# A constant matmul moved from the first to the last place of its accumulation chain

## The reference, cut to what matters

```
h   = max(layernorm(x), 0)                       # x: (64, 128, 128)
h_k = einsum('bjf,kfo->kbjo', h, W)              # W: (3, 128, 128)
out = adj_diag @ h_0 + adj_upper @ h_1 + adj_lower @ h_2 + bias
x   = x + out
```

## Time and profile before

| | us |
|---|---|
| median of 3 runs | 425.54 |
| lowest, highest | 425.4, 428.08 |
| the profiled execution | 425.69 |
| its span in the profile | 423.6 |
| TensorE busy | 408.0 |
| VectorE, ScalarE busy | 329.6, 279.7 |

### The profile page before, as it was taken

How to read it: one execution, slowest core, us unless ns; L and a number is a source line. 1 busy time by engine, 2 the same in 40 slices (tenths; PEclk the granted TensorE clock), 3 DMA queues, 4 the chain that set the end, 5 groups by cost and what they waited for, 6 DMA issues and landing times.

```text
span 423.6 us, 7808 instructions
## 1 busy us (share of the span) xinstructions
PE 408.0 (96%) x2594; PEld 365.4 (86%) x2594; DVE 329.6 (78%) x845; ACT 279.7 (66%) x566; POOL 47.7 (11%) x55
## 2 busy tenths in 40 slices
PE   8997989899999999999989999999999999999897
PEld 7785879898878899999868889999887889999787
DVE  5569898989886788797967678878888777767841
ACT  4667666775966576766776576677596676667542
POOL 3792002001100002000210001100110000000300
PEclk9998999999999999999999999999999999999999
DMA  7900000000001000000001000000000000000011
GB/s 218 373 32 0 2 0 2 1 2 0 2 19 39 14 0 15 1 20 2 0 2 38 31 0 12 1 19 0 1 2 19 27 0 14 0 20 0 13 52 63
DMA packets 6081, 11.17 MB, mean 26 GB/s; under 512 B 1056, under 2 KB 4768, under 8 KB 5536
## 3 DMA queue, kind: packets, MB, share of 16 engines
q1 hardware_dynamic: 6048, 10.77, 7.2%
HBM read 6.57 MB, written 4.19 MB: 25 GB/s over the span
## 4 chain that ended last, share of the span: by engine, by line
PE 82%; DVE 9%; ACT 4%; issue 2%; DMA 1%; POOL 1%; SPq 0%; DVEq 0%; ACTq 0%
PE PS L461 11%; PE PS L462 11%; PE PS L470 11%; PE PS L530 9%; PE PS L489 6%; PE PS L486 6%; PE PS L485 6%; PE PS L513 5%; PE PS L394 3%; PE PS L417 3%; PE PS L409 3%; PE PS L427 3%; ACT GT L709 2%; PE PS L499 1%; ACT TC L718 1%
## 5 line engine op out<-in xcount | busy, mean ns | idle before, releaser
L709 ACT ACTIVATE GT<-PS,BG 128x256 f32<-128x256 f32 (+2 forms) x312 | 158.8, 563 | 51.6 <-PE PS L489 28.2
L461 PE MATMUL PS<-HH,WIH 128*128 128x256 f32 (+2 forms) x312 | 108.8, 349 | 6.2 <-issue 2.9
L462 PE MATMUL PS<-HH,WIL 128*128 128x256 f32 (+2 forms) x312 | 103.3, 332 | 0.0
L470 PE MATMUL PS<-HL,WIH 128*128 128x256 f32 (+2 forms) x294 | 97.4, 331 | 0.3
L718 ACT ACTIVATE TC<-CS 128x512 f32<-128x512 f32 (+2 forms) x88 | 45.1, 512 | 45.9 <-DVE CS L829 29.5
L461 PEld LDWEIGHTS PS<-HH,WIH 128*128 128x128 f32 x312 | 59.2, 190 | 11.3 <-DVE HH L853 3.5
L320 POOL TENSOR_TENSOR RS<-VE,NHALF 128x8 f32<-128x8 f32 (+2 forms) x15 | 26.5, 1765 | 350.7 <-DVE VE L777 350.7
L462 PEld LDWEIGHTS PS<-HH,WIL 128*128 128x128 f32 x312 | 59.5, 191 | 3.5
L470 PEld LDWEIGHTS PS<-HL,WIH 128*128 128x128 f32 x294 | 55.6, 189 | 6.0 <-DVE HL L868 1.7
L489 PE MATMUL PS<-SL,WHH 128*128 128x256 f32 (+2 forms) x192 | 59.9, 312 | 0.0
L486 PE MATMUL PS<-SH,WHL 128*128 128x256 f32 (+2 forms) x192 | 59.8, 311 | 0.0
(11 more groups left out here) (85 smaller groups left out, 593.3 us busy)
## 6 DMA issues: line engine op xcount, KB each, us to landing
X<-x_tbd SPq DMA_DIRECT2D x3, 1024.0 KB, 11.6
out_tbd<-X SPq DMA_DIRECT2D x15, 192.0 KB, 1.9
X<-x_tbd SPq DMA_DIRECT2D x4, 256.0 KB, 4.4
WI<-wih_t SPq DMA_DIRECT2D x1, 1024.0 KB, 6.0
out_tbd<-X SPq DMA_DIRECT2D x7, 128.0 KB, 1.7
WH<-whh_t SPq DMA_DIRECT2D x1, 768.0 KB, 7.3
out_tbd<-X SPq DMA_DIRECT2D x1, 256.0 KB, 2.4
WL<-w_l SPq DMA_DIRECT2D x1, 192.0 KB, 7.0
```

Of the source, the lines that this page charges most:

```text
L461: pe.matmul(dst, WIH[:, p - 1, cols], x_high, start=True, stop=False)
L462: pe.matmul(dst, WIL[:, p - 1, cols], x_high, start=False, stop=False)
L470: mm = pe.matmul(dst, WIH[:, p - 1, cols], x_low, start=False, stop=(j == 0))
L709: act.activation(GT[:, s, q, 0:n], bank(s, q)[:, 0:n], ACT.Tanh if q == C else ACT.Sigmoid, bias=BG[:, 4 * (p - 1) + q:4 * (p - 1) + q + 1 ...
```

## The change

The bias matmul of a chunk is issued behind the chunk's last OUTP matmul instead of ahead of its first one. `start=True` goes to the first matmul of the chunk's first batch, and `out_mm` to the bias matmul. There are 24 bias matmuls in the program before and after, of the same shapes.

```diff
             def last_out(g, n, ps, plan):
 
                 c, first, last = chunk_of(plan, n)
-                if first:
+                pe.wait_ge(uk_sb, G * g + n + 1)
+                for k in range(ADJ_PARTS):
+                    pe.matmul(as_batches(ps)[:, n - plan.chunks[c][0], :], UK[:, n % 4, k * T:(k + 1) * T],
+                              WL1[:, k, :], start=(first and k == 0), stop=False, skip_group_check=True)
+                if last:
 
                     size = plan.chunks[c][1]
                     pe.matmul(as_batches(ps)[:, 0:size, :], TWO[:, :],
-                              BIAS2[:, :].unsqueeze(1).broadcast_to([T, size, D]), start=True, stop=False,
-                              skip_group_check=True)
-                pe.wait_ge(uk_sb, G * g + n + 1)
-                for k in range(ADJ_PARTS):
-                    mm = pe.matmul(as_batches(ps)[:, n - plan.chunks[c][0], :], UK[:, n % 4, k * T:(k + 1) * T],
-                                   WL1[:, k, :], start=False, stop=(k == ADJ_PARTS - 1), skip_group_check=True)
-                if last:
-                    mm.then_inc(out_mm, 1)
+                              BIAS2[:, :].unsqueeze(1).broadcast_to([T, size, D]), start=False, stop=True,
+                              skip_group_check=True).then_inc(out_mm, 1)
```

## The result

| | before | changed |
|---|---|---|
| median of 20 runs | 425.58 us | 427.31 us |
| lowest, highest | 424.74, 428.08 | 426.25, 429.79 |
| ratio of the times | | 1.0038 (95%: 1.0022 to 1.0054) |
| profiled execution, its span | 425.69, 423.6 | 429.79, 427.7 |

The changed kernel is 0.4% slower, 1.6 us, where 0.87 us was forecast: inside the stated range and inside 1%, but nearly twice the size. The interval of the ratio stands for 0.9 to 2.3 us. The profiled execution of the changed kernel happens to be its slowest, 4.1 us above that of before; 2.88 us of these are there before the first piece of the last layer is issued, where the two programs do the same. So the comparison has to be made from the first ADJP on.

What follows compares the result with a forecast made beforehand. TensorE was taken as the bound, busy 408.0 of 423.6 us. Chunk 4's 0.36, chunk 5's 0.51 and 0 elsewhere gave +0.87 us, 426.56 on the profiled execution and 426.4 us for the median; range 425.0 to 427.8 us.

Steps and rivals of the forecast that it cites:

- Chunk 4: Bias hidden in the wait before unit 9's gates becomes bare behind OUTP 12: 3 x 0.12 = +0.36 us.
- Chunk 5: Bias hidden by the wait ahead of ADJP 15 becomes bare behind OUTP 15: 3 x 0.17 = +0.51 us.
- Chunks 0 and 1: Chunk 0's bias loses its cover, +0.17 us; chunk 1's opening stall on the bank goes, -0.19 us; together taken as 0.
- Chunks 2 and 3, and LATE's single batch: Bias taken out and put back in the same dense TensorE stream: cost 0.
- The double wait: Matmul opening a chunk now waits for `out_ready` (or a gate's activation) and `uk_sb` at once: taken as 0, bound +1.1 us.
- The tail: Last group and LATE's last chunk: bias moves inside an idle stretch or a gapless TensorE stretch, cost 0.
- Nothing at all: Rival, chance 0.18: slack the chain does not show takes up the 0.29 us per group; 425.6 us.
- Faster: Rival, chance 0.12: chunk 1's stall goes (3 x 0.19), chunk 0's cover costs nothing, chunks 4 and 5 absorbed; 425.0 us.
- Slower by chunk 0: Rival, chance 0.14: chunk 0's bias loses cover and chunk 1's stall stays, 3 x 0.17 = 0.51 more; 426.9 us.
- slower by the double wait: Rival, chance 0.06: each chunk opening costs a step of 0.07 us, +1.1 + 0.87; 427.5 us.

Runs made afterwards that it cites:

- late chunks: Bias moved behind the chunk only in the two chunks per group issued in units 9 to 16 (6 of 24), against the kernel before: median 427.11 us, ratio 1.0011.
- the others: Bias moved behind the chunk in the other 18 of 24 matmuls only, against the kernel before: median 426.26 us, ratio 1.0009.
- leaving the matmuls out: Kernel before without 9 hidden bias matmuls (chunks 0, 4, 5; LATE 0, 3, 4): median 428.41 us; without 8 dense ones: 425.20 us.
- chunk 0 alone: Bias moved behind the chunk only in chunk 0 of each of the three groups, against the kernel before: median 428.04 us, ratio 1.0029.
- the filled kernels: Kernel before and changed kernel, each with unread matmuls (12 and 6) added in two TensorE waits of the first group: medians 425.36 and 426.46 us.

## Why the prediction was right or wrong

The direction held, and the mechanism held but for chunk 3 and LATE's single batch. A bias matmul that had filled a wait costs its full time at a place where TensorE is the chain, and one moved within a dense stretch costs nothing as long as nothing behind it was waiting under its cover; the split into late chunks and the others, and leaving the matmuls out, show it from both sides.

**Chunk 4**, +0.12 us in each group: measured 0.12 us, with the idle time at the old place grown from 0.23 to 0.34 us.

**Chunk 5**, +0.17 us in each group: the amount held (0.17 us), the place of the loss did not. I said that the wait ahead of ADJP 15 would grow. It stayed at 0.42 us, and the loss is at the first gate of unit 15, which waits for VectorE's HH and HL. In the trace of before these matmuls followed OUTP 13 with no idle time shown, since the bias had just about filled the gap. In group 3 the step is 0.20 us; the repeated trace of before differs by 0.03 us at this place.

**Chunks 0 and 1**, +0.17 and -0.19 us: measured +0.17, and -0.35 us at the opening of chunk 1, of which 0.17 us come back at its end. The start of ADJP 2 did not move at all. The run with chunk 0 alone gives +0.01 us in sum. VectorE's add stayed where it was (8.58 us), as I had said.

**Chunks 2 and 3, and LATE's single batch**, taken as 0: this term was mis-sized. It is 0.05 us for chunk 3 in each of two groups, since the copy of UK 10 was covered by the bias, and another 0.04 to 0.05 us at LATE's single batch. There my reading of the trace was wrong: the chain of before does not stay a bare 0.06 us in that bias (0.23 us scaled from 512 to 128 columns) but 0.29 us, with a wait for the bank in it.

```profile
329.63 0.29 PE PS L525
```

In the changed kernel this bias takes 0.06 us, and the gate matmul behind it 0.28 instead of 0.23 us; the opening waits as before. Leaving it out altogether was worth 0.05 us. That its cost was partly hidden in the wait fits these figures, but no run isolates it. For chunk 3 I had read the chunks as dense from the chain, which names only the engine; the margin of a copy against the OUTP that reads it has to be taken from the timeline of both engines. With the 384-column matmul at 0.18 instead of 0.17 us behind an fp32 matmul, the whole is 1.0 us without the step at group 2 instead of 0.87, and 1.10 us by the filled kernels.

**The double wait**, taken as 0: the changed program has 16 instructions more on its page (7,824 against 7,808), all of them EVENT_SEMAPHORE on TensorE (66 against 50) and as many as there are openings with two waits; with the late chunks alone it is 6 more, with the others 10. So the rule of the Trainium skill ("Perfetto Trace Analysis", Identifying Dependency Chains) holds here as to the instruction. Its price was nothing that can be seen: OUTP 3 takes 0.68 us and OUTP 6 0.67 us, as much as an OUTP with one wait.

**The tail**, 0: measured 0.00 us.

**The rivals.** "Nothing at all" is excluded by the filled kernels. "Faster" needed ADJP 2 to start earlier, and it did not. "Slower by chunk 0" falls by its own test, since the add of chunk 0 did not start later, and by the run with chunk 0 alone; "slower by the double wait" by the openings.

**The rest of the 1.6 us.** With the clock held, the change costs 1.10 us and not 1.6. The first comparison left 0.9 to 2.3 us open, so 1.10 us is no contradiction to it. What is above it I put down to which runs fell on the low levels of the clock: half of those of the changed kernel (16 of 32) and a third of those of before (43 of 128), a difference as large as chance gives about one time in ten. It is shown that the drop of the clock comes before the first moved matmul and that with the waits filled the cost is 1.10 us; that the unequal share is chance is likely and not proved, and at the level 0.996 the two kernels still differ by 1.5 us. That the first measured median, 427.31 us, lies inside the range is in part luck: of the forecast's cases only the double wait reached so high (427.5 us), and it did not happen.

## What to carry to other kernels

Before moving an instruction on an engine that is the chain most of the time, ask of both places whether the engine waits there: work in a wait is free, the same work in a dense stretch costs its full time, and it can be read from the two traces to some 0.05 us by the lag of common instructions. Ask also what the moved work was covering: a copy may just have been done in time behind it. A matmul that needs no late input belongs at the front of its accumulation, where it can be issued into whatever wait there is. Where the times of one program lie on levels, look at the granted clock per window first, and fill or level out what causes it before judging half a per cent.

## What the runs showed of the hardware that was not expected

Two waits of TensorE, 2.9 to 3.8 us at 33 us and 1.5 us at 55 us, go with over 3 us of this kernel's time: the clock is at 1.2 GHz for about 3 to 7 us behind the first, in five of the ten unfilled traces a second time behind the other, and the runs spread over 4.5 us. Eighteen matmuls of no use, put into these two waits, bring the spread down to 0.74 us and the median by 0.79 us, from 426.15 to 425.36 us.

At the return of VectorE's loop ahead of group 2 the chain has 1.7 us of "issue" that is 0.1 to 0.2 us longer in 5 of the 14 traces. For two programs with two traces each it is longer in one trace and not in the other, so no edit causes it.
